# One VectorE pass less in the weight quantization loop: multiply and add of a 128x1024 tile in one instruction

## The reference, cut to what matters

```python
x = x + attn(layernorm(x), w_qkv, w_proj)
x = x + ffn(layernorm(x), kernel, bias)

def fake_quant(x, bits, axes):            # bits = 8
    qmax = 2.0 ** (bits - 1) - 1.0
    amax = jnp.max(jnp.abs(x), axis=axes, keepdims=True)
    scale = jnp.where(amax > 0, amax / qmax, jnp.ones_like(amax))
    return jnp.clip(jnp.round(x / scale), -qmax, qmax) * scale
def ffn(x, kernel, bias):
    xq, kq, bq = fake_quant(x, 8, -1), fake_quant(kernel, 8, 0), fake_quant(bias, 8, -1)
    return fake_quant(relu(xq @ kq + bq), 8, -1)
```

## Time and profile before

| | us |
|---|---|
| median of 2 runs (938.54 and 939.85) | 939.2 |
| the profiled execution | 935.88 |
| its span, core 3, the slowest | 934.3 |
| spans of the eight cores | 923.6 to 934.3 |
| DVE busy in the span | 576.1 (62%) |
| PE busy in the span | 694.5 (74%) |

### The profile page before, as it was taken

One profiled execution on the slowest core, in us unless ns is written; L12 is line 12 of the kernel. 1 busy time (PEld: TensorE's weight loads), 2 busy tenths in 40 slices (PEclk: granted clock), 3 DMA queues, 4 the chain that ended last, 5 costly groups with the idle time before them and its releaser, 6 DMA issues.

```text
span 934.3 us, 11091 instructions; the slowest of 8 cores (923.6 to 934.3 us)
## 1 busy us (share of the span) xinstructions
PE 694.5 (74%) x3584; PEld 339.5 (36%) x3584; DVE 576.1 (62%) x949; ACT 337.3 (36%) x395; POOL 111.6 (12%) x93
## 2 busy tenths in 40 slices
PE   1157999899999999975555579854965746988880
PEld 0033444344444444434444334420432323433340
DVE  3352344445545545345555459983688996999997
ACT  3365343334434334345666512110211234333320
POOL 1000111111111111100000000012000000112314
PEclk9998999999999999995555579985887867999995
DMA  9552979989999997828222353379312110111122
GB/s 150 149 181 28 86 90 144 150 120 148 157 149 165 146 152 70 82 54 260 45 36 34 42 197 111 95 152 168 78 51 79 58 45 1 46 46 46 46 89 90
DMA packets 116984, 94.20 MB, mean 101 GB/s; under 512 B 101184, under 2 KB 101312, under 8 KB 113856
## 3 DMA queue, kind: packets, MB, share of 16 engines
q0 software_dynamic: 103680, 33.56, 36.8%
q1 hardware_dynamic: 13248, 59.94, 18.8%
HBM read 118.65 MB, written 8.39 MB: 136 GB/s over the span
## 4 chain that ended last, share of the span: by engine, by line
DVE 23%; PE 11%; issue 10%; DMA 5%; ACT 4%; DVEq 1%; POOLq 0%; POOL 0%; ACTq 0%; SPq 0%
DMA wpb<-wpT 4%; PE pF L535 3%; DVE bnbuf L588 2%; DVE ktb L685 2%; PE pF L343 2%; DVE kti L691 2%; DVE ktb L688 2%; DVE xr L554 2%; PE pH L334 2%; ACT aTTbuf L368 2%; ACT V8buf L362 2%; DVE ttile L798 2%; DVE cols L653 1%; PE pH L317 1%; PE pF L324 1%
## 5 line engine op out<-in xcount | busy, mean ns | idle before, releaser
L286 PE MATMUL pF<-aT,wqb 128*128 128x512 bf16 x736 | 279.8, 380 | 4.7 <-DMA wqb<-wqkvT 4.7
L288 PE MATMUL pF<-aT,wqb 128*128 128x512 bf16 x736 | 279.7, 380 | 0.0
L499 PE MATMUL pF<-wpb,sT 128*128 128x512 bf16 x256 | 107.9, 421 | 26.5 <-DMA wpb<-wpT 22.4
L535 PE MATMUL pF<-qk,xqs 128*128 128x512 bf16 x512 | 118.6, 395 | 3.7 <-ACT xqs L884 3.7
L502 PE MATMUL pF<-wpb,sT 128*128 128x512 bf16 x256 | 108.1, 422 | 0.0
L286 PEld LDWEIGHTS pF<-aT,wqb 128*128 128x128 bf16 x736 | 72.2, 98 | 93.2 <-issue 7.1
L288 PEld LDWEIGHTS pF<-aT,wqb 128*128 128x128 bf16 x736 | 72.2, 98 | 87.0 <-issue 0.8
L301 POOL DMA_DIRECT2D wqb<-wqkvT x48 | 55.0, 1146 | 338.2 <-PE pF L288 248.3
L113 DVE CAST qT<-pF 128x512 bf16<-128x512 f32 x16 | 42.7, 2668 | 69.3 <-PE pF L288 55.8
L113 DVE CAST vT<-pF 128x512 bf16<-128x512 f32 x16 | 42.7, 2672 | 59.5 <-PE pF L288 59.5
L114 ACT COPY qk<-pH 128x512 bf16<-128x512 bf16 x64 | 34.0, 590 | 116.7 <-PE pH L478 116.7
(11 more groups left out here) (117 smaller groups left out, 870.4 us busy)
## 6 DMA issues: line engine op xcount, KB each, us to landing
wqb<-wqkvT POOLq DMA_DIRECT2D x48, 512.0 KB, 10.3
ktc<-wkT SPq DMA_DIRECT2D x32, 512.0 KB, 8.5
ktb<-wkT SPq DMA_DIRECT2D x32, 512.0 KB, 3.6
xbuf<-x_att SPq DMA_DIRECT2D x8, 1024.0 KB, 7.3
xr<-x_res SPq DMA_DIRECT2D x8, 1024.0 KB, 7.6
wpb<-wpT POOLq DMA_DIRECT2D x32, 256.0 KB, 6.2
out<-xr SPq DMA_DIRECT2D x7, 1024.0 KB, 3.8
bias_b<-bias SPq DMA_DIRECT2D x1, 1024.0 KB, 4.8
```

What stands on the lines that cost most here:

```text
L286: tn.matmul(pa[:, :], wch, aT[:, 1024 * c:1024 * c + 512], start=st, stop=sp)
L288: mm = tn.matmul(pb[:, :], wch, aT[:, 1024 * c + 512:1024 * c + 1024], start=st, stop=sp)
L499: tn.matmul(pF[2 * (idx % 2)][:, :], lhs, wpb[:, 1024 * m:1024 * m + 512], start=st, stop=sp)
L535: mm = tn.matmul(pF[u][:, :], xqs[Mt % 2][:, 128 * c:128 * (c + 1)], qk[:, 2048 * c + 512 * u:2048 * c + 512 * (u + 1)], start=(c == 0), s ...
```

## The change

Lines 685 and 688 become one instruction, which multiplies by the reciprocal scale and adds MAGIC. The wait between the two (`selfV`) goes with the second. The same buffers are read and written, and nothing else is changed. It applies to all 32 tiles.

```diff
@@ -682,11 +682,9 @@
                 v.wait_ge(S_(f"fKt2{i % 2}"), 16 * (i // 2 + 1))
                 wt(v, h_sk[ft])
-                h_qa = inc(v.tensor_scalar_mul(ktb[i % 2][:, :], ktb[i % 2][:, :],
-                                               cols[:, 64 + ft:65 + ft]), "selfV")
-                wt(v, h_qa)
-                h_qb = inc(v.tensor_scalar_add(ktb[i % 2][:, :], ktb[i % 2][:, :],
-                                               MAGIC), "selfV")
+                h_qb = inc(v.tensor_scalar(ktb[i % 2][:, :], ktb[i % 2][:, :],
+                                           cols[:, 64 + ft:65 + ft], MAGIC,
+                                           ALU.mult, ALU.add), "selfV")
                 wt(v, h_qb)
                 h_kv = inc(v.tensor_scalar(kti[i % 2][:, :], ktb[i % 2][:, :],
                                            MAGIC, None, ALU.subtract), "fKv")
```

## The result

The changed kernel takes 0.9799 of the time before (95% interval 0.9774 to 0.9825; 938.47 us before in the same runs): 18.9 us less, by the interval 16.4 to 21.2. The forecast was 19.7 us less. That the kernel is faster is clear; whether by more than 2% is not, since the interval lies on both sides of 0.98. The median over all its runs, 922.4 us, contains disturbed ones, which the ratio leaves out. The profiled execution took 919.73 us.

A forecast was written before the change was run, and what follows sets the result against it. No engine bounds the whole span: DVE, nearly tied with PE, holds tiles 0 to 13, the weight load 14 to 19, DVE 20 to 31. 10.1 + 0 + 9.6 = 19.7 us; 939.2 - 19.7 = 919.5 us, range 914.5 to 924.

The forecast's parts named there:

- A tile saves 0.80 us: Each of 32 loop tiles: fused instruction takes 749 ns, a tile falls from 3.13 to 2.33 us.
- The rival in which the fused instruction costs as much as the two: Every tile: fused instruction takes 0.86 + 0.80 us, no saving, 939.2 us; chance 0.03.
- Stretch A: Tiles 0 to 13, until POOL may load the second weight half: 10.1 us saved of 11.2.
- The tie between DVE and PE: Projection step 7, the gate of POOL's load: DVE allows 599.7, PE 599.9, equal within 0.2 us.
- Stretch B: Tiles 14 to 19, during the second weight half's load: saves 0, as the load keeps its 42.0 us.
- The rival of a shorter load: Second weight half's load 2.3 us shorter as two tile loads lie before it, 917.2 us; chance 0.11.
- The rival of a longer load: Second weight half's load 2.9 us longer, 922.4 us; chance 0.17, shared with a later PE.
- Stretch C: Tiles 20 to 31, after the load: DVE goes tile to tile, 12 x 0.80 = 9.6 us saved.
- Behind the loop: After DVE's arrival at 753.00 the shift passes to the end: 0, with 1 us either way.
- The lower clock: Projection steps 1 to 7: TensorE stays at its lower clock, 15.6 us a step, 970 us; chance 0.03.

The follow-up runs named there:

- e1: Kernel before with the fused instruction in tiles 0 to 13 only, two passes kept in the others; ratio 0.9889 to the kernel before.
- e2: Kernel before with the fused instruction in tiles 14 to 19 only, two passes kept in the others; ratio 0.9995 to the kernel before.
- e5: Changed kernel with two extra passes that compute nothing in each of tiles 14 to 19; ratio 0.9787 to the kernel before.
- e3: Kernel before with the fused instruction in tiles 20 to 31 only, two passes kept in the others; ratio 0.9916 to the kernel before.
- e6: Changed kernel with a second pair fused, line 689's subtraction and line 694's multiplication; ratio 0.9645 to the kernel before.
- e7: Changed kernel, but POOL may load each part of the second weight half once projection step 7 has read it; ratio 0.9746 to the kernel before.
- e10: Changed kernel with tile 20's load alone held back until the projection weight is complete; ratio 0.9788 to the kernel before.

## Why the prediction was right

**A tile saves 0.80 us: right.** 749 ns for the fused instruction and 2.33 us for a tile, both as forecast. The rival in which the fused instruction costs as much as the two is out. It was what the Trainium skill's "VectorE: DVE Perf Modes" (section "Rules for kernel authors") would give by the first half of its rule, "Don't try to fuse for perf"; its second half, to keep the number of ops small, is what the change does, and the trace agrees with that half: here two adjacent pairs were fused, and each took 0.8 us off a tile wherever DVE was the bound.

**Stretch A, 10.1 us: right.** Means 72.8 to 62.6, that is 10.2; e1 shows that these 14 tiles alone do it. The tie between DVE and PE came out as a tie: which engine is late last differs by core. On cores 3 and 6 PE waits for nothing once its first steps are through; on the others DVE is late by some 0.3 to 0.5 us at step 7. PE on core 0, against the earlier trace rows:

```profile
561.08 1.06 PE L478 MATMUL pH<-ident,kqb 128*128 128x128 bf16 x16
...
568.88 1.06 PE L478 MATMUL pH<-ident,kqb 128*128 128x128 bf16 x16
...
601.75 0.38 PE L499 MATMUL pF<-wpb,sT 128*128 128x512 bf16 x1 [0.33 <-DVE xr L554]
```

The steps follow each other at PE's own 7.80 us (561.08 to 568.88), and DVE is late again only at the end, by 0.12 us at step 6 and 0.33 at step 7. On core 1, DVE first and then PE:

```profile
547.83 0.75 DVE L685 TENSOR_SCALAR ktb<-ktb,cols 128x1024 f32<-128x1024 f32 x1 [3.70 <-DMA ktb<-wkT]
```

```profile
570.48 0.38 PE L499 MATMUL pF<-wpb,sT 128*128 128x512 bf16 x1 [0.20 <-DVE xr L554]
```

Tile 2 waited 3.70 us for its load, so DVE is late from step 4 on (PE's line above), and A is 63.5 us there against 62.2 on core 3. The forecast gave up 0.8 us to the first tiles' waits; on cores 1 and 7 it is more.

**Stretch B, 0: right, and its cause better known now.** 41.4 to 40.9. e2 and e5 show that six tiles' work may be cut by 4.8 us or raised by 9.6 with no effect. The reason given, that the load keeps its length, holds for the change but not in general. The rival of a shorter load had the right mechanism, tile loads that slip ahead of it. At this change one does, tile 17's (2.46 to 2.30 MB in B), and B is 0.5 us shorter in the means, which is no more than B varies among kernels with the same tiles in it (e1 40.0, e3 40.8, before 41.4); at e6 it was worth 2.8. The rival of a longer load did not come (42.7 us on core 0, the slowest after, 40.9 in the mean). That the cores' loads draw on a shared memory, as the prediction read from cores 3 and 7, no run tests.
That DVE passes keep GpSimd from writing descriptors, as "SBUF — State Buffer" of the Trainium skill has it, would have made B some 1 us shorter by the estimate in the prediction, and e5's twelve added passes would have made it longer; e5's B differs by 0.3 us, within what B varies between cores. Single issues still take up to 921 ns instead of 531; no run shows a price for the load in that.

**Stretch C, 9.6 us: right, 0.3 too much.** 93.4 to 84.1 in the changed kernel, 83.7 in e3. Neither PE nor a load came late. Of the 0.4 us between the two the traces show the place and not the reason: the pause between lines 685 and 689 of tile 29, on core 0:

```profile
719.46 0.69 DVE L689 TENSOR_SCALAR kti<-ktb 128x1024 int32<-128x1024 f32 x1 [0.46 <-DVE ktb L685]
```

It is 0.46 us on every core of the changed kernel and 0.11 in e3, which makes up the difference; the instruction waits for line 685 of its own tile in both.

**Behind the loop, 0: right within its 1 us.** The tail is 181.9 us against 181.4, and between 181.3 and 182.6 in all the kernels, whatever they change ahead of it.

**The lower clock: it did not happen.** The granted clock in A, from 561 us on, was 1.00 before and after, and 0.88 in C after 0.86.

The sum of the means is 10.2 + 0.5 + 9.3 - 0.4 = 19.6 us, less 0.7 for a later first tile: 18.9, as by the mean spans and by the ratio. The forecast's 919.5 lies within 0.1 us of 0.9799 of 938.47, 919.6. That exactness is luck: the profiled execution alone gave 16.1 us, and the slowest core moved from core 3 to core 0, by when each core began the loop.

## What to carry to other kernels

Count the instances of a shortened step by what waits behind them, not all together: here 14 of 32 paid 10.2 of their 11.2 us, 12 paid 9.3 of 9.6 and 6 paid nothing, and the neighbouring engine's own turn (PE's 7.80 us against DVE's (600.33 - 558.90) / 5 = 8.3) told how much a second cut of the same kind could bring. Here a stretch that is bound by transfers was shortened by moving other transfers out of it, not by faster compute in its shadow. Two dependent `tensor_scalar` passes over one f32 tile are worth fusing where the engine that runs them holds the path.

## What the runs showed of the hardware that was not expected

Stretch B, in which the core's DMA engines are busy some 90% of the time, paid for the other transfers in it: 1.9 us per tile load of 512 KB by e6 and e7, 3.1 us for the one taken out in e10, where a tile load took 3.6 us from issue to landing in the median over the whole kernel before. Inside B on core 0 of the changed kernel one takes 10.6 us in the median. The transfer for which nothing waits is not free: taken out of B, it gave back half of the 3.6 us or more.
